# The feed-forward bias leaves TensorE: VectorE adds it, masked and gated by token, to the residual tile

## The reference

```python
x = x + attn_a(layernorm(x))     # 32 heads, softmax
x = x + ffn(layernorm(x))        # phase 3 of the kernel
x = x + attn_b(layernorm(x))     # 4 heads, causal sigmoid attention, q/k/v by sign vectors
x = x + ffn(layernorm(x))        # the last stage
```

```python
hits = softmax(x @ centroids.T / 0.1) > 0.01      # tokens x 64 clusters
query_sel = any(hits, axis=1)                     # per token
row_sel = any(hits, axis=0)[assignments]          # per output column, over all tokens
out = where(query_sel[:, None] & row_sel[None, :], x @ weight.T + bias, 0)
```

## Time and profile before

| | |
|---|---|
| median of 3 runs | 3414.24 us (3413.55 to 3415.07) |
| profiled execution | 3413.33 us, span 3411.6 us |
| mean granted TensorE clock | 0.986 |
| busy: PE, DVE, ACT, POOL | 3211.6, 2173.1, 1776.3, 1864.7 us |
| matrix products | 24256 |

### The profile page before, as it was taken

How to read it: one execution, slowest core, us unless ns; L and a number is a source line. 1 busy time by engine, 2 the same in 40 slices (tenths; PEclk the granted TensorE clock), 3 DMA queues, 4 the chain that set the end, 5 groups by cost and what they waited for, 6 DMA issues and landing times. The chain is left out here.

```text
span 3411.6 us, 62568 instructions
## 1 busy us (share of the span) xinstructions
PE 3211.6 (94%) x24256; PEld 1705.5 (50%) x24256; DVE 2173.1 (64%) x3858; ACT 1776.3 (52%) x2125; POOL 1864.7 (55%) x2065
## 2 busy tenths in 40 slices
PE   0899999999999999999997699998999999999999
PEld 0355555555555555555553355554455555554443
DVE  8377777777777777777777587775455555542311
ACT  3277777777777777777775422221345555552000
POOL 2377777777777777777664322221555555540422
PEclk9999999999999999999997799999999999999999
DMA  4122222222222222222223454443222222213533
GB/s 185 41 60 72 64 71 72 71 69 66 69 64 72 63 76 69 69 70 59 59 59 100 159 168 159 154 163 119 79 81 99 100 100 104 95 75 142 198 141 136
DMA packets 272869, 330.36 MB, mean 97 GB/s; under 512 B 91677, under 2 KB 206365, under 8 KB 271551
## 3 DMA queue, kind: packets, MB, share of 16 engines
q1 hardware_dynamic: 267902, 309.57, 28.6%
q10 hardware_dynamic: 4608, 16.78, 1.2%
q0 software_dynamic: 64, 0.01, 0.0%
HBM read 191.52 MB, written 134.22 MB: 95 GB/s over the span
## 5 line engine op out<-in xcount | busy, mean ns | idle before, releaser
L652 DVE TENSOR_REDUCE nmax<-ring_ps 128x1 f32<-128x512 f32 x1024 | 686.8, 688 | 417.4 <-PE ring_ps L484 414.0
L758 POOL TENSOR_TENSOR elo<-e,ehi 128x1024 f16<-128x1024 f32 x256 | 615.9, 2406 | 432.5 <-ACT ehi L598 425.1
L533 PE MATMUL proj_ps<-xnT,arena 128*128 128x512 f16 x3072 | 750.2, 380 | 3.3 <-DVE xnT L697 2.5
L592 ACT ACTIVATE e<-st_ps,exp_scale 128x1024 f32<-128x1024 f32 x512 | 571.4, 1116 | 344.3 <-PE st_ps L494 260.9
L598 ACT ACTIVATE ehi<-st_ps,exp_scale 128x1024 f16<-128x1024 f32 x512 | 570.1, 1114 | 64.7 <-PE ctx_ps L514 57.1
L533 PEld LDWEIGHTS proj_ps<-xnT,arena 128*128 128x128 f16 x3072 | 299.5, 98 | 373.0 <-ACT stage L610 10.6
L1527 PE MATMUL f_ps<-wT,fxT 128*128 128x512 f16 x1920 | 434.3, 380 | 2.9 <-DMA fxT<-xT_scratch 2.9
L494 PE MATMUL st_ps<-qs,ks 98*128 98x512 f16 x1024 | 396.8, 387 | 16.6 <-ACT ehi L598 10.0
L511 PEld LDWEIGHTS ctx_ps<-v_sb,ehi 128*128 128x128 f16 x4096 | 313.6, 98 | 192.8 <-DVE sums L679 81.5
L484 PE MATMUL ring_ps<-ks,qs 96*128 96x512 f16 x1024 | 401.1, 392 | 8.4 <-DVE nmax L652 8.2
L511 PE MATMUL ctx_ps<-v_sb,ehi 128*128 128x65 f16 x4096 | 374.6, 193 | 30.6 <-DVE sums L679 20.7
(11 more groups left out here) (238 smaller groups left out, 4655.9 us busy)
## 6 DMA issues: line engine op xcount, KB each, us to landing
qk_scratch<-qk_hl SPq DMA_DIRECT2D x128, 256.0 KB, 2.3
fxT<-xT_scratch SPq DMA_DIRECT2D x64, 512.0 KB, 3.5
qs<-qk_scratch SPq DMA_DIRECT2D x192, 128.0 KB, 2.7
ks<-qk_scratch SPq DMA_DIRECT2D x192, 128.0 KB, 2.9
arena<-x_scratch SPq DMA_DIRECT2D x48, 512.0 KB, 4.4
ctx_scratch<-ctx SPq DMA_DIRECT2D x64, 256.0 KB, 3.1
ct<-ctx_scratch SPq DMA_DIRECT2D x32, 512.0 KB, 4.8
xb<-in_L_attn_a_x_dram SPq DMA_DIRECT2D x32, 512.0 KB, 4.5
```

The lines of the kernel that those rows point to most:

```text
L533: mm = pe.matmul(proj_ps[:], wqk[:, wp, c, H * qk + P * g:H * qk + P * g + P], xnT[:, b % 2, xp, c, :], start=(n == 0), stop=(n == 23))
L592: nc.scalar.activation(e32[:, half], st_ps[:, half], ACT.Exp, scale=exp_scale[:, 0:1]).then_inc(e32_done, 1)
L652: dve.tensor_reduce(nmax[:, h % 2, c:c + 1], ring_ps[:, ring_max(h, c) % 2, :], AX.X, ALU.max, negate=True).then_inc(ring_free, 1)
L758: nc.gpsimd.tensor_tensor(elo[:, h % 2, 2:4, :], e32[:, 1], ehi[:, h % 2, 2:4, :], ALU.subtract).then_inc(elo_pool, 1)
```

## The change

TensorE's bias product goes, and the 24th product closes the sum. The bias row is loaded on all 128 partitions (`fbm`) instead of 33, its split and its part in the scale go, and `hit_rows` no longer waits for its load. At the start of phase 3 VectorE multiplies `fbm` by the column mask. For each token tile of rows 0 to 7 VectorE then does `x2 = fbm * qsel + x2` on 128x1024 (`add_bias`), placed behind `evict` at j = 2 and 6 and at heads 0 and 2; GpSimd's `add_ffn` waits for it (`pre_done`). `evict` and the others take their scalar from a separate `inv_f`, and `qsel` stays a plain 0 or 1. For the second feed-forward the bias row is loaded again and multiplied by the second mask, and each of the 32 tiles gets the addition in the last stage (`add_bias4`): that of tile 8 + v/2 behind `scaled_direct(v)` for even v, that of tile v - 1 between the two `scaled_raw` for v = 1 to 8. `hit_rows` now shares its memory with a work buffer of phase 3 (`y32c`), so it is stored to DRAM at the end of phase 2 and loaded again ahead of the second mask.

```diff
-            hit_rows = sb(p234, "hit_rows", [NC, H], F16)
+            y32c = sb(p234, "y32c", [P, 512])
+            hit_rows = y32c[0:NC].bitcast(F16)
-            fb_hl = sb(p234, "fb_hl", [33, H], F16)
-            ones33 = sb(p234, "ones33", [33, P], F16)
+            fbm = sb(p234, "fbm", [P, H])
...
-                        sp.dma_start(fbx[:], fb.partition_broadcast(33)).then_inc(row_in2, 16)
+                        sp.dma_start(fbm[:], fb.partition_broadcast(P)).then_inc(fb_in, 16)
...
+                        sp.wait_ge(rows_set, 1)
+                        sp.dma_start(hit_d, hit_rows).then_inc(hit_out, 16)
                         sp.wait_ge(bind, BOUND)
...
-                        dve.wait_ge(row_in2, 48)
+                        dve.wait_ge(row_in2, 32)
...
+                        sp.wait_ge(pre_done, T * B)
+                        sp.dma_start(fbm[:], fb.partition_broadcast(P)).then_inc(fb4_in, 16)
+                        sp.wait_ge(mask_full, 2)
+                        sp.wait_ge(y_lo, 8 * B)
+                        sp.dma_start(hit_rows, hit_d).then_inc(hit_in, 16)
                         for o in range(NB4):
                             load_x4(o)
...
-                                pe.matmul(f_ps[:, half, :], fxT[:, t % 2, xp, c, :], wT[:, wp, c, cols], start=(n == 0), stop=False)
+                                mm = pe.matmul(f_ps[:, half, :], fxT[:, t % 2, xp, c, :], wT[:, wp, c, cols], start=(n == 0), stop=(n == 23))
                             if z == 24:
-                                pe.matmul(f_ps[:, half, :], ones33[:], fb_hl[:, cols], start=False, stop=True).then_inc(f_full, 1)
+                                mm.then_inc(f_full, 1)
...
                         pe.wait_ge(csel_done, 2)
                         pe.wait_ge(sig, 16 * B)
+                        pe.wait_ge(hit_in, 16)
...
+                        dve.tensor_tensor(fbm[:], fbm[:], mask[:], ALU.mult).then_inc(fbm_done, 1)
+                        dve.wait_ge(fbm_done, 1)
+
+                        def add_bias(b, t):
+                            if not row(b):
+                                return
+                            n = T * b + t
+                            dve.wait_ge(x1_in[n % NX], 16 * (n // NX + 1))
+                            dve.scalar_tensor_tensor(out=x2_tile(b, t), in0=fbm[:], scalar=qsel[:, 0, n:n + 1], in1=x2_tile(b, t),
+                                                     op0=ALU.mult, op1=ALU.add).then_inc(pre_done, 1)
...
                                     evict(b + 1, j // 2 - 1)
+                                    if j != 4:
+                                        add_bias(b + 1, j // 4)
...
                                 evict(b + 1, 4 + hd)
+                                if hd % 2 == 0:
+                                    add_bias(b + 1, 2 + hd // 2)
...
+                        def add_bias4(k):
+                            o = turn_of[k]
+                            dve.wait_ge(x4_in[o % NB4], 16 * (o // NB4 + 1))
+                            dve.scalar_tensor_tensor(out=x4_tile(k), in0=fbm[:], scalar=qsel[:, 1, k:k + 1], in1=x4_tile(k),
+                                                     op0=ALU.mult, op1=ALU.add).then_inc(pre4_done, 1)
+
+                        scaled_direct(0)
+                        dve.wait_ge(fb4_in, 16)
+                        dve.tensor_tensor(fbm[:], fbm[:], mask[:], ALU.mult).then_inc(fbm_done, 1)
+                        dve.wait_ge(fbm_done, 2)
+                        add_bias4(RAW)
+                        for v in range(1, DIRECT):
                             scaled_direct(v)
-                            if 1 <= v <= RAW:
+                            if v % 2 == 0:
+                                add_bias4(RAW + v // 2)
+                            if v <= RAW:
                                 scaled_raw(2 * v - 2)
+                                add_bias4(v - 1)
                                 scaled_raw(2 * v - 1)
...
-                            pool.wait_ge(x1_in[n % NX], 16 * (n // NX + 1))
+                            pool.wait_ge(pre_done, n + 1)
...
-                            pool.wait_ge(x4_in[o % NB4], 16 * (o // NB4 + 1))
+                            pool.wait_ge(pre4_done, bias_of[k] + 1)
```

More of the change, by code:

```diff
@@ L136, in hybrid_layer @@
     V1 = 2 * HD + 1
+    hit_d = nc.dram_tensor("hit_scratch", (NC, H), F16).ap()
     ctx_d = nc.dram_tensor("ctx_scratch", (B * G, T, P, P), F32).ap()
@@ L955, in _ @@
                         sp.wait_ge(cq_in, 32)
+                        sp.wait_ge(fb_in, 16)
+                        sp.wait_ge(hit_out, 16)
                         for i in range(4):
@@ L1153, in weight_max @@
                                 return
[L1154 to L1158 removed]
+                            dve.wait_ge(fw_max, C)
+                            dve.tensor_reduce(m1[:, 2:3], mx[:], AX.X, ALU.max).then_inc(max2, 1)
                         def weight_scale(k):
@@ L1164, in weight_scale @@
                             scale_from_absmax(dve, m2[:, 2:3], e_w[:, 2:3], sc[:, 2:3], sc2, 3)
-                        def lo_bias():
-                            dve.wait_ge(fb_hi, 2)
-                            dve.scalar_tensor_tensor(out=fb_hl[32:33], in0=fbx[32:33], scalar=sc[32:33, 2:3], in1=fb_hl[32:33],
-                                                     op0=ALU.mult, op1=ALU.subtract)
                         def lo_weights(k):
@@ L1381, in hybrid_layer @@
                 NB4, RAW = 8, 2 * T
+                pre_done, pre4_done, fbm_done, fb4_in, hit_in = (sem(n) for n in ("pre_done", "pre4_done", "fbm_done", "fb4_in", "hit_in"))
                 x4_in = [sem(f"x4_in{i}") for i in range(NB4)]
@@ L1396, in hybrid_layer @@
                 turn_of = {k: o for o, k in enumerate(order4)}
+                biased4 = [k for v in range(DIRECT) for k in ([] if v % 2 else [RAW + v // 2]) + ([v - 1] if 1 <= v <= RAW else [])]
+                bias_of = {k: i for i, k in enumerate(biased4)}
                 def x4_tile(k):
@@ L1543, in ffn_direct @@
                                 c, (xp, wp) = i // 3, ((0, 0), (0, 1), (1, 0))[i % 3]
-                                pe.matmul(f4_ps[v % 4], fxT[:, n % 2, xp, c, :], wT[:, wp, c, cols], start=(i == 0), stop=False)
-                            pe.matmul(f4_ps[v % 4], ones33[:], fb_hl[:, cols], start=False, stop=True).then_inc(f_full, 1)
+                                mm = pe.matmul(f4_ps[v % 4], fxT[:, n % 2, xp, c, :], wT[:, wp, c, cols], start=(i == 0), stop=(i == 23))
+                            mm.then_inc(f_full, 1)
                         def scores_b(b, hd):
@@ L1877, in scaled_raw @@
                             dve.scalar_tensor_tensor(out=fm[:, p % 2], in0=x2[:, (T * B + k) % NX, 512 * half:512 * half + 512],
-                                                     scalar=qsel[:, 1, k:k + 1], in1=mask[:, 512 * half:512 * half + 512],
+                                                     scalar=inv_f[:, k:k + 1], in1=mask[:, 512 * half:512 * half + 512],
                                                      op0=ALU.mult, op1=ALU.mult).then_inc(fm4_done, 1)
```

32 lines of the change are left out of this document (7 added, 25 removed).

## The result

The changed kernel takes **3371.34 us** (median of 4 runs, 3370.41 to 3371.80), the kernel before, in the same session, 3413.89 (4 runs, 3413.21 to 3415.07): ratio 0.9876, 95% interval 0.9864 to 0.9889. The profiled span is 3369.8 us (before 3411.6), the mean granted TensorE clock 0.985.

What follows compares the result with a forecast made beforehand. The prediction took TensorE to bound the kernel from phase 3 on. Its stage-by-stage terms summed to -25.5 us, giving 3387.8 us, or 3388.7 against the median, with a range of 3372 to 3407.

Steps and rivals of the forecast that it cites:

- Bound and gross gain: From phase 3 on TensorE bounds; 128 bias products at 0.42 or 0.47 us each are 54 to 60 us gross.
- last rival: Neighbours' longer start has another cause and stays, so each product frees only 0.216 us: 3408, chance 0.04.
- The addition: VectorE's 64 additions of 128x1024 float32 take 1.27 us each, waits for GpSimd apart; upper bound 2.73.
- rival "slower": An addition takes 2.34 us or more, with 27 on the path: 3418, or 3426 with GpSimd's turns; chance 0.10.
- Term 5: First half of steps b = 0 to 6: the j = 6 addition delays xhT, +1.8 us each, making steps nearly neutral.
- term 4: Second half (heads) of steps b = 0 to 6: four products gone, -1.9 us a step, two additions hidden.
- The pieces of b = 0: Eight half tiles of step b = -1 gain 3.4 us; the first half of b = 0, without a wait, loses 0.6.
- Terms 1, 2 (phase 2): Start of phase 2 freed from the bias row's load, -2 us; the assignment rows' store at its end, +0.6.
- term 2: End of phase 2: the assignment rows' store stands ahead of the cq round trip, +0.6 us, between 0 and 1.
- Terms 7, 8 (burst): Last stage: v = 0 to 2 gain 1.3 us; v = 1 to 8, rounds of 6.2 and 7.1, lose 2.4.
- What would prove me wrong: Steps shorter by more than 2 us, an addition never below 2, or blocks 9 to 13 keeping 5.2.
- all of it is gained: VectorE's queue hides every addition and burst rounds stay below 5.9 us: gain 46 to 52, 3362 to 3368; chance 0.10.

Runs made afterwards that it cites:

- e1: The changed kernel with all 64 bias additions left out (output lacks the bias): 3364.20 us, ratio 0.9852.
- e7: The kernel before, products kept, with only the bias row's load on its own semaphore so hit_rows no longer waits for it: 3409.76 us, ratio 0.9985.
- e6: The changed kernel with the eight raw-tile additions moved from the last stage to step b = 8, nothing left out: 3364.75 us, ratio 0.9857.
- e3: The changed kernel without the addition at j = 2, that at j = 6 kept: 3388.73 us, ratio 0.9924.
- e9: The changed kernel without its 64 additions, and with lo_v3 moved ahead of evict at j = 6: 3353.95 us, ratio 0.9823.
- e4: The changed kernel without the addition at j = 6, that at j = 2 kept: 3360.17 us, ratio 0.9843.
- e5: The changed kernel with lo_v3 moved from j = 6 to behind the last xhT, nothing left out: 3361.89 us, ratio 0.9846.
- e10: The changed kernel without the addition at j = 2, and with the one at j = 6 moved ahead of evict: 3378.10 us, ratio 0.9894.

## Why the prediction was wrong, by its own steps

- **Bound and gross gain: right.** TensorE bounds phase 3 and the tail, a product costs twice its own 0.216 us: 35 blocks at 0.42 us made -14.7 predicted, -14.7 measured. The last rival (half of it stays with the neighbours) is out.
- **The addition: right.** 1.27 us taken, 1271 to 1284 measured in 41 of the 64. The rule at half throughput, quoted from the Trainium skill's Vector Engine (DVE) Microarchitecture Reference, would have it at some 2.5 us (an estimate, twice the 1.27); the 2.3 to 2.5 us that do occur stand where GpSimd is at work, as at 3165.09. The rival "slower" is out with it. (It is the third rival, not the last, that the prediction's text on this rule means.)
- **Term 5, the first halves of the steps: the step that failed.** It said +1.8 us each. Measured is -2.49 a step for the whole, less the heads' -1.88 of term 4: -0.6. The error of 2.4 us has two parts.
  - (a) The stretch in which the scores hang on VectorE begins only at the transposes of j = 5. From their end to the scores it was 10.01 us (2677.15 to 2687.16 before) and is 10.34 (2665.23 to 2675.57 after). All that lies outside this stretch, six of a step's eight products, passes through at 0.47: -2.82, of which -0.94 belongs to the first half. My term names "what the earlier start gives back" but puts no number on it.
  - (b) The stretch itself grew by 0.33 and not by 1.8, because I kept GpSimd's `lo_v` where the trace of before had it, 0.95 us ahead of VectorE. I did not see that the products' going brings VectorE nearer to it by 0.94 (e1), nor follow what the addition of j = 2 does to GpSimd. I had even written that this addition "falls into a gap": VectorE's gap, not the port's (it takes 2.46 us there).

  Over b = 1 to 7 both parts make the 14.6 us (b = 7 has no addition and misses by 0.6 alone).
- **The pieces of b = 0** went the other way: -2.8 predicted, -1.2 measured. In this step both operations collide, the addition at 2.49 us and `lo_v3` at 2.17, and the wait that I said this step does not have appears: 1.6 us lost. So a loss of the kind that term 5 forecast for seven steps occurs in full in one.
- **Terms 1, 2 (phase 2): right in sign**, -2.0 for -1.4; e7 gives the first of them as -2.7 by itself (taken: -2). The size is no finer than the scatter of this phase, 446.3 to 449.7 us with the same code. No run takes the store of term 2 by itself.
- **Terms 7, 8 (burst): right within 1 us.** Rounds of 5.98 and 6.96 us for 6.2 and 7.1; `scaled_direct(9)` done 56.0 us after the mask for 57.2. The place and the cause are shown by e6: without the eight raw additions no wait is left.
- **Phase 1** is 1.3 us shorter although nothing of it changed. Over the kernels of this case it ends between 1914.5 and 1917.8 us, so I take this part of the gain for scatter between kernels.
- **What would prove me wrong** had "steps shorter by more than 2 us (VectorE hides it)". The first half of that happened, the reason in brackets is not it: e1 and e3 show that the additions are not hidden but change an order.

The rival "all of it is gained" (3362 to 3368, chance 0.10) came nearer in time than my forecast, by another way: with the burst's 5.3 us and, against e9's 79.88, 1.4 us of each middle step lost, and with the old collision gone.

## What to carry to other kernels

Where VectorE and GpSimd share a port, count the time between the starts of their two-input operations, not only their lengths: who was first by 0.02 us decided 2 us per step, and repeated itself in every step. Work taken from a third engine shifts the two against each other, too: here 0.94 us. An operation added on one engine can pay for itself, or its removal cost time, by changing who comes first; so follow the other engine's start times through the added work before sizing a collision, and try the order of two neighbours on the chip. And let a saved product pass through up to the last point on which the critical wait really hangs.

## What the runs showed of the hardware

- Who is issued first holds the port for its whole length, by margins as small as 0.01 to 0.03 us: behind GpSimd's 2.13 us `lo_v`, VectorE's 1.22 us `lo_v3` takes 3.18 us (e1), ahead of it 1.21 (e9). The Trainium skill's SBUF — State Buffer, "Who interferes with whom", says that issue order and not the shape of the operation decides who blocks; these two runs agree.
- GpSimd's smallest operations wait as well: L118 on 128x1, 0.27 us alone, took 1.89 us behind addition and `lo_v3` (2672.48 in the changed kernel).
- Waits of TensorE up to 2.3 us left the granted clock at 1.00 (no slice of 4 us between 2450 and 3010 below it in the changed kernel, e1, e4, e5 or e9). Longer ones went both ways: at head 0 of b = 0 a wait of 2.75 us left it at 1.00 in the changed kernel and one of 2.77 was followed by 0.73 over 4 us in e6; behind 3.01 us it stayed in two of five steps and fell in three, to 0.57 over 4 us in one (e10). Behind 4.38 us it was 0.70 over 4 us and lower in the next steps (e3). What tells equal waits apart was not tried.
- Who goes next when one already waits is not settled. VectorE's second operation passed the waiting L118 (2673.10 in the changed kernel), but GpSimd's waiting L1939 went ahead of `lo_v3` (2676.13 in e3). No run takes apart whether the form of the instruction or the moment of its issue does this.
- `scalar_tensor_tensor` with two float32 tiles of 128x1024 in SBUF runs at the same 1.27 us as with float32 and float16.
